# Four binned gather chunks merged into three tiles of a block, and three dense chunks instead of four, in a sparse aggregation

## The reference

```python
xn = _layernorm(x, axis=-1)
x = x + segment_sum(edge_weight[:, None] * xn[dst], src, 6250) + mix(xn)
x = x + moe(_layernorm(x, axis=-1))     # 8 experts, the best 2 of each node
```

## Time and profile before

| | us |
|---|---|
| median of three runs | 2134.69 |
| the profiled execution | 2141.8 |
| its span | 2140.0 |
| PE busy | 1966.1 |
| DVE busy | 1396.4 |
| ACT busy | 1227.2 |
| POOL busy | 1284.5 |

### The profile page before, as it was taken

How to read it: one execution, slowest core, us unless ns; L and a number is a source line. 1 busy time by engine, 2 the same in 40 slices (tenths; PEclk the granted TensorE clock), 3 DMA queues, 4 the chain that set the end, 5 groups by cost and what they waited for, 6 DMA issues and landing times. The chain is left out here.

```text
span 2140.0 us, 36257 instructions
## 1 busy us (share of the span) xinstructions
PE 1966.1 (92%) x11866; PEld 1725.6 (81%) x11866; DVE 1396.4 (65%) x2564; ACT 1227.2 (57%) x3610; POOL 1284.5 (60%) x1281
## 2 busy tenths in 40 slices
PE   5788789999999999999999999999999993799994
PEld 2476678998899889988998899889989993688773
DVE  6885378758875887588758875887577677300113
ACT  4641055566556655665566566655666662577673
POOL 1000577667766776677667766776666650477774
PEclk9898989999999999999999999999999996799997
DMA  7522543333322332333223322332333333134456
GB/s 247 193 74 84 193 143 123 124 113 102 94 88 91 102 96 88 92 101 95 89 90 101 97 87 92 101 94 89 91 112 115 116 109 97 57 122 140 139 179 226
DMA packets 131071, 245.40 MB, mean 115 GB/s; under 512 B 26645, under 2 KB 78628, under 8 KB 130888
## 3 DMA queue, kind: packets, MB, share of 16 engines
q0 software_dynamic: 59584, 161.78, 24.5%
q1 hardware_dynamic: 64860, 74.91, 10.6%
q10 hardware_dynamic: 6444, 6.40, 0.9%
HBM read 198.18 MB, written 45.77 MB: 114 GB/s over the span
## 5 line engine op out<-in xcount | busy, mean ns | idle before, releaser
L1206 POOL DMA_INDIRECT edge_G<-xn_scratch,edge_row_i x1029 | 1029.4, 1000 | 460.1 <-issue 240.1
L1309 ACT ACTIVATE edge_weighted<-edge_hots,bins_scale 128x128 f32<-128x128 bf16 x2401 | 738.4, 391 | 60.7 <-DVE edge_row_hots L1366 60.7
L1272 PE MATMUL edge_op<-edge_G,edge_weighted 128*128 128x256 f32 x2058 | 515.4, 387 | 15.2 <-DVE all_xn L1379 13.1
L1300 ACT COPY edge_A<-edge_ap 128x512 f32<-128x512 f32 x343 | 201.1, 586 | 568.3 <-PE edge_ap L1259 568.3
L1361 DVE TENSOR_TENSOR edge_hots<-edge_numbers,bins_recb 128x1024 bf16<-128x1024 bf16 x343 | 236.6, 690 | 310.2 <-PE edge_ap L1259 308.3
L1272 PEld LDWEIGHTS edge_op<-edge_G,edge_weighted 128*128 128x128 f32 x2058 | 364.9, 191 | 55.2 <-DVE all_xn L1379 16.5
L1259 PEld LDWEIGHTS edge_ap<-edge_weighted,edge_row_hots 128*128 128x128 f32 x2744 | 355.8, 192 | 38.6 <-issue 16.6
L1259 PE MATMUL edge_ap<-edge_weighted,edge_row_hots 128*128 128x128 f32 x2744 | 363.1, 275 | 14.0 <-ACT edge_weighted L1309 8.4
L1276 PE MATMUL edge_op<-bins_win,edge_A 128*128 128x256 f32 x1568 | 371.6, 380 | 0.0
L1276 PEld LDWEIGHTS edge_op<-bins_win,edge_A 128*128 128x128 f32 x1568 | 298.9, 191 | 41.0
L1276 PE MATMUL edge_op<-edge_win,edge_A 128*128 128x256 f32 x1176 | 277.8, 379 | 0.0
(11 more groups left out here) (313 smaller groups left out, 1996.1 us busy)
## 6 DMA issues: line engine op xcount, KB each, us to landing
edge_G<-xn_scratch,edge_row_i POOLq DMA_INDIRECT x1029, 2.8
exp_ys<-ys_scratch SPq DMA_DIRECT2D x12, 1024.0 KB, 6.0
ln_xin<-in_x SPq DMA_DIRECT2D x12, 512.0 KB, 5.7
xn_scratch<-ln_xnb ACTq DMA_DIRECT2D x12, 512.0 KB, 6.2
xnT_scratch<-ln_xT SPq DMA_DIRECT2D x12, 512.0 KB, 6.7
mix_xg<-xn_scratch SPq DMA_DIRECT2D x12, 512.0 KB, 3.8
mix_ek<-xnT_scratch SPq DMA_DIRECT2D x12, 512.0 KB, 4.6
mix_xg<-in_x SPq DMA_DIRECT2D x12, 512.0 KB, 3.8
```

The costliest lines, as they stand in the source:

```text
L1206: pool.indirect_dma_start(out=G[:, t % AHEAD, i, :], out_offset=None, in_=xn_dram, in_offset=bass.IndirectOffsetOnAxis(ap=row_i[:, q % 2, ...
L1272: nc.tensor.matmul(op[j][:, :], weighted[:, j, i, :], G[:, rb, i, :], start=i == 0, stop=False)
L1300: nc.scalar.copy(A[:, j, :, :].rearrange("p c s -> p (c s)"), ap[j][:, :]).then_inc(a_kept, 1)
L1309: last = nc.scalar.activation(weighted[:, t % 2, i, :], hots[:, t % 2, i // 2, :, i % 2], ACT.Copy, scale=scale[:, b, i:i + 1])
```

## The change

Four chunks of a group (`KG` = 4, 34 tiles each) are now binned as gather chunks, three (`DN` = 3) as dense ones; the last group has 30, 29, 29 and 29 tiles in the first four. Behind the binning, DVE merges the slots of the four chunks of a block into three tiles of 128 (`GN` = 3) without gaps between the chunks. Each chunk's slots start where the chunk before ended (`offset`, counted by a new product on PE), modulo 128 (`wrap`); every (chunk, partition) pair belongs to one of four tiles (`tile_of`), and a tile is the bitwise or of what belongs to it (`mask`, `picked`, `paired`, `merged`). The fourth tile, what doesn't fit into three, is put into the first tile of the same block in the next group. If more than 128 edges of a block are left over, or one chunk has more than 128 for a block, the flag is set. The steps then see 3 gather and 3 dense tiles: 6 one-hots, 6 weighings, 3 gathers, 3 `ap` and 6 `op` products. The new work has its own step for the offsets, so that all later parts come one step later (`SLOT_AT` 10, `HALF_AT` 14, `UNPACK_AT` 47); the row numbers are ready at n = 37 instead of 28.

```diff
-GN, DN = 3, 4
-CB = GN + DN
+KG, GN, DN = 4, 3, 3
+CB = KG + DN
+SC = GN + DN
-REAL = (35, 35, 34, 30, 30, 30, 30)
-LP, SP2 = 18, 15
+LP, SP2 = 17, 15
+REAL = (2 * LP,) * KG + (2 * SP2,) * DN
+LAST_REAL = (30, 29, 29, 29) + (2 * SP2,) * DN
...
-    NE = DN + GN + 1
+    NE = SC
...
+    OFF_AT = BASE_AT + 1
+    SLOT_AT = OFF_AT + 1
...
-    ROWS_AT = KEEP_AT + 4 * (GN - 1) + 1
+    MERGE_AT = KEEP_AT + 4 * (KG - 1) + 1
...
@@ pe_share, at BASE_AT
+            for h in range(2):
+                nc.tensor.matmul(self.count_of, self.ones[:, :],
+                                 self.before[:, LP, 0:KG, :, h].rearrange("p c b -> p (c b)"), start=h == 0, stop=h == 1)
...
@@ dve_share
+        if n == self.OFF_AT:
+            dve.wait_ge(self.based, q + 1)
+            offset, counts = self.offset, self.count_of.rearrange("p (k b) -> p k b", k=KG)
+            for k in range(KG):
+                self.next_link(dve, q, nc.vector.tensor_tensor(offset[:, k + 1, :], offset[:, k, :], counts[:, k, :], ALU.add))
+            self.next_link(dve, q, nc.vector.tensor_copy(self.offset_i[:, :, :], offset[:, 0:KG, :]))
+            nc.vector.tensor_single_scalar(self.first_i[:, :, :], self.offset_i[:, :, :], P - 1, op=ALU.bitwise_and)
+            self.next_link(dve, q, nc.vector.tensor_single_scalar(self.tile_i[:, :, :], self.offset_i[:, :, :], 7,
+                                                                  op=ALU.arith_shift_right))
+            self.next_link(dve, q, nc.vector.scalar_tensor_tensor(self.tile_of[:, :, :], self.first_i[:, :, :],
+                                                                  self.part[:, 0:1], self.tile_i[:, :, :],
+                                                                  ALU.is_gt, ALU.add))
+            left = FULL if q + 1 < NQ else FULL - P
+            self.next_link(dve, q, nc.vector.tensor_scalar_add(self.over[:, :], offset[:, KG, :], -float(left)))
+            nc.vector.tensor_scalar_max(offset[:, 0, :], self.over[:, :], 0.0)
...
+                    if k < KG:
+                        self.next_link(dve, q, nc.vector.tensor_scalar(self.wrap[:, :, :], self.slot[:, :, k, :], float(P),
+                                                                       -float(P), ALU.is_ge, ALU.mult))
+                        self.next_link(dve, q, nc.vector.tensor_tensor(self.slot[:, :, k, :], self.slot[:, :, k, :],
+                                                                       self.wrap[:, :, :], ALU.add))
...
-        if n == self.ROWS_AT:
...
+        if n == self.MERGE_AT:
+            dve.wait_ge(self.kept, q * CB + KG)
...
+        m = n - self.MERGE_AT - 2
+        if 0 <= m <= GN:
+            one = self.merged[:, :, m, :]
+            self.next_link(dve, q, nc.vector.tensor_scalar(self.mask[:, :, :], self.tile_of[:, :, :], float(m), -1.0,
+                                                           ALU.is_equal, ALU.mult))
+            self.next_link(dve, q, nc.vector.tensor_tensor(
+                self.picked[:, :, :, :].rearrange("p f k b -> p f (k b)"),
+                self.found[:, :, :, :].rearrange("p f k b -> p f (k b)"),
+                self.mask[:, :, :].rearrange("p (a k) b -> p a (k b)", a=1).to_broadcast([P, 3, KG * NB]),
+                ALU.bitwise_and))
+            self.next_link(dve, q, nc.vector.tensor_tensor(
+                self.paired[:, :, :, :].rearrange("p f k b -> p f (k b)"),
+                self.picked[:, :, 0:2, :].rearrange("p f k b -> p f (k b)"),
+                self.picked[:, :, 2:4, :].rearrange("p f k b -> p f (k b)"), ALU.bitwise_or))
+            self.next_link(dve, q, nc.vector.tensor_tensor(one, self.paired[:, :, 0, :], self.paired[:, :, 1, :],
+                                                           ALU.bitwise_or))
+            if m == 0:
+                self.next_link(dve, q, nc.vector.tensor_tensor(one, one, self.merged[:, :, GN, :], ALU.bitwise_or))
+            if m == GN - 1:
+                if q > 0:
+                    dve.wait_ge(self.rows_taken, q)
+                nc.vector.tensor_scalar_min(self.next_rows[:, :, :], self.merged[:, 0, 0:GN, :].rearrange("p k b -> p b k"),
+                                            float(N - 1)).then_inc(self.rows_ready, 1)
...
@@ dve_decode
-        nc.vector.tensor_copy(self.recb[:, :, 0:CB], self.src_of[:, :, :].rearrange("p k b -> p b k"))
+        for a, b, node, weight in ((0, GN, self.merged[:, 1, 0:GN, :], self.merged[:, 2, 0:GN, :]),
+                                   (GN, SC, self.src_of[:, KG:CB, :], self.weight_of[:, KG:CB, :])):
+            nc.vector.tensor_copy(self.recb[:, :, a:b], node.rearrange("p k b -> p b k"))
+            nc.vector.tensor_copy(self.scale[:, :, a:b], weight.bitcast(F32).rearrange("p k b -> p b k"))
```

More of the change, by code:

```diff
@@ L109 @@
     FARTHEST = 254
-    NE = DN + GN + 1
+    NE = SC
+    assert NE % 2 == 0
     HALVES = 2 * CB
-    HOTS = CB + sum(r % 2 for r in REAL)
+    HOTS = CB
     HOT_AT = 0
@@ L153, in __init__ @@
         self.slot = st.sb("slot", [P, LP, CB, 2], BF16)
-        self.most = st.sb("most", [P, NQ])
+        self.wrap = st.sb("wrap", [P, LP, 2], BF16)
+        self.offset = st.sb("offset", [P, KG + 1, NB])
+        self.over = st.sb("over", [P, NB])
+        self.offset_i = st.sb("offset_i", [P, KG, NB], I32)
+        self.first_i = st.sb("first_i", [P, KG, NB], I32)
+        self.tile_i = st.sb("tile_i", [P, KG, NB], I32)
+        self.tile_of = st.sb("tile_of", [P, KG, NB], I32)
+        self.mask = st.sb("mask", [P, KG, NB], I32)
+        self.found = st.sb("found", [P, 3, KG, NB], I32)
+        self.picked = st.sb("picked", [P, 3, KG, NB], I32)
+        self.paired = st.sb("paired", [P, 3, 2, NB], I32)
+        self.merged = st.sb("merged", [P, 3, GN + 1, NB], I32)
+        self.most = st.sb("most", [P, 3 * NQ])
         SL = st.sb("SL", [P, 2 * HP * P * 2], BF16)
@@ L436, in dve_share @@
+            self.next_link(dve, q, ins)
+            self.next_link(dve, q, nc.vector.tensor_tensor(self.total[:, KG:CB, :], before[:, SP2, KG:CB, :, 1],
+                                                           self.start[:, KG:CB, :, 1], ALU.add))
+            self.next_link(dve, q, nc.vector.tensor_reduce(self.most[:, 3 * q + 2:3 * q + 3],
+                                                           self.total[:, KG:CB, :].rearrange("p c b -> p (c b)"),
                                                            AX.X, ALU.max))
@@ L1307, in weigh @@
                         act.wait_ge(stepped, t - 1)
-                    for i in (*range(GN, CB), *range(GN)):
+                    for i in (*range(GN, SC), *range(GN)):
                         last = nc.scalar.activation(weighted[:, t % 2, i, :], hots[:, t % 2, i // 2, :, i % 2], ACT.Copy,
@@ L2295, in gps_layer @@
         with Stage(nc, "bins") as bs:
-            bins = Bins(nc, bs, above, iota49, iota128, ident, low_i)
+            bins = Bins(nc, bs, above, iota49, iota128, part, ident, low_i)
             norm_stage(nc, x, W_qk[1], b_qk[1], src_t, dst_t, ew_t, xn_dram, xnT_dram, keyT, gmax, ident, bins)
```

143 lines of the change are left out of this document (77 added, 66 removed).

## The result

The changed kernel takes 1992.79 us as the median of four runs (1989.69 to 1995.19) against 2135.2 of the kernel before: ratio 0.9329, 95% interval 0.9311 to 0.9347. The forecast was 2019, and its range began at 1998: faster, as forecast, and by 26 us more. The profiled execution took 1989.69.

What follows compares the result with a forecast made beforehand. TensorE was taken to bound the edge stage, with POOL next at 194.1 us a group. 2141.8 - 93.8 (six groups) - 30 (last group) + 8 (mixing stage) = 2026, less 7.1 gives 2019 us; range 1998 to 2056.

Steps and rivals of the forecast that it cites:

- mixing stage: Before the edge groups: offsets and merge add DVE work on the path, +8 us, bounds 0 and +14.5.
- six groups, by POOL's copies: Edge stage, between POOL's row-number copies: 1272.8 us become 6 x 196.5 = 1179, so -93.8.
- from that decode to the last addition: Last group, routing instead of binning: 48 x 0.655 us less 1 for the border comes through, -30.
- POOL: 196 us a group: Edge groups: POOL's 194.1 us plus 2 of merge stalls passes PE's 178.5 and cuts off the saving.
- the 0.5 on top of it: Edge groups: loss where two nearly equal paths, 194 and 196 us, meet; 196.5 us a group taken.
- POOL's free pace: Edge groups: 147 x (1.009 + 0.305) = 193.1 us plus row-number copy and the wait behind it, 194.1 a group.
- The merge's stalls: Gathers on POOL held up by VectorE's merge operations: 2 us a group taken, bounds nothing and 8.
- The path without POOL: Edge groups: the path through DVE and PE sums to 194 us a group, against POOL's 196.
- PE's stall at the border: Between groups, PE waiting at decode: grows from 0.93 to about 1.5 us as its cover shrinks.
- The clock: Sign of error: TensorE's clock leaving 1.00 would show the forecast wrong.
- the rival's half clock: Edge steps: PE waits for gathers; half clock makes steps 6.5 us instead of 3.75, up to 2288 us; 3%.
- VectorE as the bound: Edge groups' merge and offset steps: VectorE bounds at 205 us a group, whole 2075 us; chance 17%.

Runs made afterwards that it cites:

- e2: Changed kernel without the third window product of each step (148 us of PE's work left out): 1984.4 us, ratio 0.9298.
- e6: Kernel before, with one dense chunk of four left out of both product loops and ACT's copy, no merge: 1980.9 us, ratio 0.9271.
- e1: Changed kernel with two of the three gathers of a step issued, the third product reading the second's rows again: 1975.5 us, ratio 0.9254.
- e4: Changed kernel without the merge operations of the four merge steps, so the fourth chunk is lost: 1976.3 us, ratio 0.9262.
- e3: Changed kernel with the slot numbers' large operations (L489) cut into pieces of two positions, whole work: 1980.2 us, ratio 0.9277.
- e5: Changed kernel with the mask, pick, pair and join operations of each merge step done twice: 2037.5 us, ratio 0.953.
- e12: Kernel before, whole work, with the slot numbers' operations in pieces of two positions: 2143.8 us, ratio 1.0036.
- e11: Changed kernel, whole work: merge spread as in e8, addition before one-hots as in e10, slot numbers' operations in pieces of one position: 1949.3 us, ratio 0.9124.
- e8: Changed kernel with the merge's parts spread to steps 33, 35, 36, 40, 42 and 43 instead of 33 to 38: 1993.7 us, ratio 0.9324.
- e7: Changed kernel without the merge operations and with the slot numbers' operations in pieces of two positions: 1944.3 us, ratio 0.9096.
- e9: Changed kernel, whole work, with the merge spread as in e8 and the slot numbers' operations in pieces of two positions: 1959.5 us, ratio 0.9173.
- e10: As e9 on the changed kernel, with DVE adding step b-2's result before making step b+1's one-hots: 1955.6 us, ratio 0.9153.

## Why the prediction was right and wrong

The mechanism held: PE loses 0.655 us a step, sinks under POOL, and the saving is cut off at POOL's pace (e2 and e6). The size was off by 36 us in the profiled execution, 1989.7 against 2026. Of these 10 go back in the medians, since the profiled execution of before lay 6.6 above its median and that of the changed kernel 3.1 below. The sum, term by term. The lag is from POOL's last copy to the decode of the last group, 1552.4 and 1432.7 us; the last term runs from there to the last addition, 1778.9 and 1626.0.

| | forecast | measured |
|---|---|---|
| mixing stage | +8 | 270.4 - 268.0 = +2.4 |
| six groups, by POOL's copies | -93.8 | -116.0 |
| the last group's decode behind POOL's copy | 0 | 11.6 to 5.5: -6.1 |
| from that decode to the last addition | -30 | 226.5 to 193.3: -33.2 |
| tail | 0 | +0.8 |
| sum | -116 | -152.1 |

The first row rests on one execution each and is the least certain. e6 leaves the mixing stage of the kernel before as it is, and there the first copy comes at 264.2; e1 and e2 leave that of the changed kernel, and theirs come at 271.4 and 271.8. So the mixing stage costs +2.4 to +7.6, and of the 6.6 us by which the profiled execution of before is slow, 3.8 may lie there. The other rows don't hang on it.

- **The term that failed is "POOL: 196 us a group", and the 0.5 on top of it; measured, 192.8.** Three parts. POOL's free pace was put at 194.1; e6 shows 192.6. About 0.3 of the difference is a gap counted twice: the 0.65 behind the copy is one of the 147 gaps and doesn't come on top of them. Another 0.4 is its length, 0.27 now. The remaining 0.9 are the gathers beside the four large operations, which take 8.6 us a group more than undisturbed ones in the kernel before and 7.7 in e6. The merge's stalls, chosen as 2 between 0 and 8, are at most 0.8 (e4, 192.0 against 192.8), and only 0.3 of it stands beside the merge's own operations. That a gather waits for the rest of the operation it starts in holds beside the four large ones (20 gathers of the five groups after the first end 0.81 to 0.82 us behind theirs), not beside every one of the merge's: 12 that start inside a `picked`, with 0.57 us of it left in the mean, are 0.05 longer. And the half microsecond for two nearly equal paths was not lost.
- **The path without POOL, summed to 194, is 191** (e1). That it lies within 2 us of POOL's was right, and it is the most useful line of the working: it explains why e1, e3 and e4 alone give so little. Its terms weren't measured one by one; one that was too high is PE's stall at the border, put at 1.5 and seen at 0.5.
- **The lag at the last border was left out.** With PE as the bound POOL was five steps ahead; now PE stands close behind it, and those 6 us are gained once.
- **The mixing stage** was put at 8 us. The merge alone costs that much there (e4, 8.3), where the sum gave it 5 and the offsets 2.9, so that the total came near is partly luck. The rest of the change gave some of it back: up to the copy of `qbias` the changed kernel is 6.2 us late (213.4 against 207.2; 204.7 in e6), in the final loop it catches up 3.8 (2.5 against e6), where DVE unpacks three chunks instead of seven. That reading of the last part is argued from the trace and wasn't tried by itself.
- **The clock** leaving 1.00 was named as a sign of being wrong. It does leave it, for some 4 us in a group after the first. No row of the working shows the rival's half clock, from which it has its 6.5 us a step and its 2288. The trace of the kernel before grants 0.50 from 1805 to 1820 us, behind the edge stage, and never in its groups after the first; in those of the changed kernel it is granted for 20 of 964 us, which is the time of 3 such steps, where the rival needed 42. It costs the groups nothing that shows, since POOL sets them: with 148 us of PE's work less (e2) the clock is 0.50 for 55 of 965 us, and the groups stay. But the 2 us a group lie on the path without POOL, which is just 2 under POOL's; what it would be without them no run shows.
- **VectorE as the bound** was given 17% at 205 a group. It isn't, but e5 shows how near it is: 7.2 us more give 6.0.
- **The range** reached down to 1998 with merge stalls and mixing at nothing. It took POOL's 194.1 as a floor without bounds of its own, which is why it missed by 5. It was worked out from a kernel in which PE set the pace, and needed an end below.

The trace of the changed kernel shows the stall of rows 5 again, with 2.88 us for a gather beside an operation of 2.65 us on VectorE, and e3 turns it into time: cutting these operations shortened the gathers from 1008 to 967 ns in the mean. What a gather waits for beside them isn't shown by any run here, nor why it doesn't wait beside some others that have both inputs in SBUF too: in the changed kernel the gathers at 726.99 and 740.74 us, each begun inside an `SL` of 1.35 us (L513), take 0.95.

Still open: what ends POOL's 0.30 us between two gathers. No run here changed it.

## What to carry to other kernels

When the bound engine gets lighter, work out the free pace of the next one from its own rows, operation by operation with the gaps between, and give it both ends: its durations were taken while it waited for somebody. Where two paths lie within a few microseconds of each other, an edit to one of them alone says little about its worth; try it together with an edit to the other (12.6 and 16.5 alone, 48.5 together, and 0 alone but 21 with the pieces). A granted clock of 0.99 over a long stretch can hide short ones at half: cut the stretch up before calling the clock steady. Long VectorE operations that stretch the gathers beside them cost nothing here while TensorE bounds (e12, where cutting them gained nothing) and cost time once GpSimd does (12.6 us, e3).

## What the runs showed of the hardware

- In the five groups after the first of the changed kernel 20 gathers start inside one of the four large operations of the slot numbers (L489, 2.65 to 3.01 us, both inputs in SBUF). All end 0.81 to 0.82 us behind it and take 2.62 to 3.16 us, the one in the fence of e3 2.88; the ten that start 0.05 or 0.06 us ahead of one take 0.94 to 0.96. With the operations cut and nothing changed on GpSimd a gather takes 967 ns in the mean with pieces of two positions (e3) and 961 with pieces of one (e11, with the merge spread), against 1008 in the changed kernel. Beside a `tensor_reduce` of 1.88 us, with one input, a gather takes its usual 0.95 (changed kernel, at 721.99 us), and so it does beside an `SL` of 1.35 us with both inputs in SBUF (L513, at 726.99 us).
- The other way: `picked` on VectorE, 0.77 us with both inputs in SBUF, took 2.96 and 2.85 beside additions of 2.35 and 2.34 on GpSimd (e8).
- With PE busy 183.6 of 193.0 us of a group, the granted clock still fell to 0.50, six times in five groups, each within 1.2 us behind a wait of PE of 1.9 to 2.1 us; eleven waits were of 1.9 to 2.15 us. In e7, e9, e10 and e11, whose waits end at 1.6 us or less, it stayed at 1.00 in the groups after the first.
